# A fused graph network on one core: graph 0 without GpSimd's units, 11 units a graph by VectorE, variance products in groups of four slots

## The reference

```python
hi = x @ W1[:H];  hj = x @ W1[H:]
h = relu(hi[:, :, None, :] + hj[:, None, :, :] + b1)   # every pair (i, j) of nodes
y = h @ W2 + b2
y = layernorm(y, gamma, beta)                          # over the features of each pair
out = einsum('bij,bijh->bih', adj, y)                  # weighted sum over j
x = layernorm(x + out)
```

## Time and profile before

| | |
|---|---|
| median of 3 runs | 2835.23 us (2824.11 to 2839.78) |
| the profiled execution, its own time | 2829.14 us |
| its span, first to last instruction | 2827.5 us |
| mean granted clock of TensorE | 0.990 of full speed |
| GpSimd busy | 2131.9 us, 75% of the span |
| mean rate of the transfers | 202 GB/s |

### The profile page before, as it was taken

One profiled execution on the slowest core, in us unless ns is written; L12 is line 12 of the kernel. 1 busy time (PEld: TensorE's weight loads), 2 busy tenths in 40 slices (PEclk: granted clock), 3 DMA queues, 4 the chain that ended last, 5 costly groups with the idle time before them and its releaser, 6 DMA issues.

```text
span 2827.5 us, 60731 instructions
## 1 busy us (share of the span) xinstructions
PE 2720.4 (96%) x10882; PEld 1133.2 (40%) x10882; DVE 2655.9 (94%) x20561; ACT 2582.0 (91%) x6916; POOL 2131.9 (75%) x3026
## 2 busy tenths in 40 slices
PE   5999999999999999999999999999999999999993
PEld 2343444444444444444434443444444444434442
DVE  1999999999999999999999999999999999999997
ACT  5999999999999999999999999999999999999991
POOL 4777877777877877777777777778777777777772
PEclk9999999999999999999999999999999999999995
DMA  2555455555545545545545554554555554555452
GB/s 81 195 205 233 192 206 232 192 197 233 201 190 233 207 188 234 208 189 224 217 188 209 227 194 191 215 224 191 211 228 191 212 227 191 203 221 206 188 211 104
DMA packets 170235, 571.71 MB, mean 202 GB/s; under 512 B 68608, under 2 KB 104320, under 8 KB 104320
## 3 DMA queue, kind: packets, MB, share of 16 engines
q1 hardware_dynamic: 169856, 567.82, 51.6%
HBM read 555.17 MB, written 8.39 MB: 199 GB/s over the span
## 4 chain that ended last, share of the span: by engine, by line
DVE 61%; DMA 26%; PE 7%; issue 3%; ACT 1%; SPq 1%; POOL 0%; DVEq 0%; POOLq 0%; ACTq 0%
DVE h L653 38%; DMA cb<-c_scratch 19%; DMA c_scratch<-c 6%; DVE h L639 5%; PE y_ps L387 5%; DVE stats L677 3%; DVE gT L653 3%; DVE x L686 3%; DVE mv L680 1%; DVE z_aff L760 1%; PE ss_ps L399 1%; DVE invs L661 1%; DVE z_aff L755 1%; DVE z L747 1%; DVE c L669 1%
## 5 line engine op out<-in xcount | busy, mean ns | idle before, releaser
L387 PE MATMUL y_ps<-h,w2c 128*128 128x512 f32 x4096 | 2041.9, 613 | 55.7 <-DVE h L639 35.5
L653 DVE CUSTOM_DVE_ANT_0 h<-h,cb 128x128 f32<-128x128 f32 x8192 | 1994.0, 288 | 91.8 <-DMA cb<-c_scratch 91.1
L892 POOL TENSOR_SCALAR h<-vT,uT 128x128 f32<-128x128 f32 x2048 | 1698.5, 843 | 174.9 <-ACT vT L516 105.7
L526 ACT ACTIVATE h<-uv_ps,uT 128x128 f32<-128x128 f32 x4800 | 1433.1, 440 | 4.5 <-DVE gT L653 4.4
L536 ACT ACTIVATE sq<-y_ps,b2c_col 128x1024 f32<-128x1024 f32 x1024 | 1191.2, 1163 | 169.1 <-PE y_ps L387 163.3
L387 PEld LDWEIGHTS y_ps<-h,w2c 128*128 128x128 f32 x4096 | 675.4, 190 | 996.1 <-issue 516.2
L653 DVE DVE_READ_ACCUMULATOR2_ANT gT<- 128x1 f32 x8192 | 629.0, 77 | 0.0
L399 PE MATMUL ss_ps<-sq,sel 128*32 128x512 f32 x4096 | 545.5, 605 | 0.0
L880 POOL TENSOR_TENSOR var_eps<-mv,eps_col 128x1 f32<-128x1 f32 x448 | 94.6, 211 | 371.8 <-DVE mv L680 369.8
L639 DVE TENSOR_SCALAR h<-vT,uT 128x128 f32<-128x128 f32 x1216 | 338.6, 292 | 5.5 <-ACT mask_all L581 3.5
L883 POOL TENSOR_TENSOR rs<-var_eps,minus_half 128x1 f32<-128x1 f32 x448 | 301.8, 674 | 35.0
(11 more groups left out here) (100 smaller groups left out, 1485.0 us busy)
## 6 DMA issues: line engine op xcount, KB each, us to landing
cb<-c_scratch SPq DMA_DIRECT2D x512, 1024.0 KB, 8.3
adj_c<-in_adj_dram SPq DMA_DIRECT2D x512, 8.0 KB
devs<-dev_rows SPq DMA_DIRECT2D x512, 8.0 KB
x_in<-in_x_dram SPq DMA_DIRECT2D x64, 64.0 KB, 10.8
c_scratch<-c SPq DMA_DIRECT2D x128, 32.0 KB, 1.5
adj_in<-in_adj_dram SPq DMA_DIRECT2D x64, 64.0 KB, 4.4
x_res<-in_x_dram SPq DMA_DIRECT2D x64, 64.0 KB, 5.2
out_dram<-x SPq DMA_DIRECT2D x64, 64.0 KB, 3.1
```

What stands on the lines that cost most here:

```text
L387: op = pe.matmul(y_ps[:, t % 2, c0:c0 + COLS], w2c[:], h[:, t, c0:c0 + COLS], start=True, stop=True)
L526: op = act.activation(h[:, t, n * P:(n + 1) * P], v, ACT.Relu, bias=uT[:, b, i:i + 1])
L653: op = dve.tensor_tensor_reduce(h[:, t, cols], h[:, t, cols], cb[:, t // 2, c0:c0 + P], 1.0, 0.0, ALU.mult, ALU.add, gT[:, i:i + 1])
L892: op = pool.tensor_scalar(h[:, t, n * P:(n + 1) * P], vT[:, b, :], uT[:, b, i:i + 1], 0.0, ALU.add, ALU.max)
```

## The change

Four things change together.

1. `vector_units(g, t)`: VectorE makes 4 units of each slot in graph 0, and in later graphs one unit in odd slots, none in even ones, and 4 in slot 15 as before: 7 + 4 = 11 a graph where there were 19. ScalarE makes the others of the first six: 6 in even slots, 5 in odd ones, 2 in slot 15, that is 85 a graph where there were 77. GpSimd still makes the last two.
2. `pool_units(g, t)`: in graph 0 GpSimd makes none, and ScalarE makes units 4 to 7.
3. `spread_coefficients`: the first chunk of a half (two slots, 1 MB) goes as two transfers of one slot each, with a semaphore of its own for the first (`cb_first`). `weighted_sum` waits for it at the first slot of a half and for the rest of the chunk at the second.
4. `variances(g, t)`: one visit for four slots (`GROUP` = 4) instead of two, 8 matmuls in a row instead of 4. `sq` becomes a ring of six slots, and its places are counted over graphs.

```diff
@@ -22,7 +22,8 @@
-SQ_RING = 4
+SQ_RING = 6
+GROUP = 4
@@ -37,19 +38,38 @@
-def vector_units(t):
-
-    return BLOCK_UNITS if t == SLOTS - 1 else 1
...
-def act_end(t):
-
-    return DUO_UNITS - (2 if early_unit(t) else 1)
+def vector_units(g, t):
+
+    if g == 0 or t == SLOTS - 1:
+        return BLOCK_UNITS
+    return t % 2
+
+
+def pool_units(g, t):
+
+    if g == 0:
+        return 0
+    return 2
...
+def act_end(g, t):
+
+    return DUO_UNITS - pool_units(g, t)
@@ -319,7 +341,13 @@
-                    sp.dma_start(cb[:, CHUNKS * half + p, :], src.partition_broadcast(P)).then_inc(cb_in[CHUNKS * half + p], 16)
+                    skip = 0
+                    if p == 0:
+                        skip = DUO_UNITS * P
+                        sp.dma_start(cb[:, CHUNKS * half, 0:skip], src[0:skip].partition_broadcast(P)
+                                     ).then_inc(cb_first[half], 16)
+                    sp.dma_start(cb[:, CHUNKS * half + p, skip:], src[skip:].partition_broadcast(P)
+                                 ).then_inc(cb_in[CHUNKS * half + p], 16)
@@ -376,13 +404,14 @@
-                    wait(pe, h_dve, SLOTS * g + t + 1)
-                    if t < SLOTS - 1:
-                        wait(pe, h_act_head, (SLOTS - 1) * g + t + 1)
+                    if vector_units(g, t) > 0:
+                        wait(pe, h_dve, vector_slots(g, t))
+                    if vector_units(g, t) < BLOCK_UNITS:
+                        wait(pe, h_act_head, head_slots(g, t))
                     wait(pe, sq_done, SLOTS * g + t - 1)
                 else:
                     wait(pe, h_act, SLOTS * g + t + 1)
-                    wait(pe, h_pool, SLOTS * g + t + 1)
+                    wait(pe, h_pool, SLOTS * (g - 1) + t + 1)
@@ -390,15 +419,17 @@
-                half, p = t // HALF, (t % HALF) // 2
-                wait(pe, sq_done, SLOTS * g + t + 2)
-                if p == 0:
+                half = t // HALF
+                wait(pe, sq_done, SLOTS * g + t + GROUP)
+                if t % HALF == 0:
                     wait(pe, dev_done, 2 * g + half)
-                for q in range(4):
-                    c0 = (q % 2) * COLS
-                    mm = pe.matmul(ss_ps[32 * q:32 * q + 32, :], sel[:, ROWS - 1 - p:ROWS - 1 - p + 32],
-                                   sq[:, (t + q // 2) % SQ_RING, c0:c0 + COLS],
-                                   start=(p == 0), stop=(p == ROWS - 1))
+                for d in range(GROUP):
+                    p = (t + d) % HALF // 2
+                    for block in range(2):
+                        q = 2 * (d % 2) + block
+                        mm = pe.matmul(ss_ps[32 * q:32 * q + 32, :], sel[:, ROWS - 1 - p:ROWS - 1 - p + 32],
+                                       sq[:, (SLOTS * g + t + d) % SQ_RING, block * COLS:(block + 1) * COLS],
+                                       start=(p == 0), stop=(p == ROWS - 1))
                 mm.then_inc(var_summed, 1)
@@ -493,8 +524,8 @@
-                    sg, t = lagging(graphs, s, START + 3)
-                    if s % 2 == 1 and sg is not None:
+                    sg, t = lagging(graphs, s, START + 1 + GROUP)
+                    if t % GROUP == 0 and sg is not None:
                         variances(sg, t)
@@ -632,18 +663,20 @@
                 if n == 0:
-                    if t % 2 == 0:
+                    if t % HALF == 0:
+                        wait(dve, cb_first[t // HALF], 16 * (g + 1))
+                    elif t % 2 == 0 or t % HALF == 1:
                         wait(dve, cb_in[t // 2], 16 * (g + 1))
```

More of the change, by code:

```diff
@@ L37, with slots_where, vector_slots, head_slots @@
 LATER_SET_UP_SLOT = 2
-def vector_units(t):
-    return BLOCK_UNITS if t == SLOTS - 1 else 1
-def early_unit(t):
-    return True
-def act_end(t):
-    return DUO_UNITS - (2 if early_unit(t) else 1)
+def vector_units(g, t):
[6 more added lines that the diff above has]
+    return 2
+def slots_where(units, g, t):
+    return sum(1 for i in range(SLOTS * g + t + 1) if units(i // SLOTS, i % SLOTS))
+def vector_slots(g, t):
+    return slots_where(lambda g, t: vector_units(g, t) > 0, g, t)
+def head_slots(g, t):
+    return slots_where(lambda g, t: vector_units(g, t) < BLOCK_UNITS, g, t)
+def act_end(g, t):
+    return DUO_UNITS - pool_units(g, t)
 def unit_of(t, n):
@@ L187, in build @@
         cb_in = [sem(f"cb_in{i}") for i in range(2 * CHUNKS)]
+        cb_first = [sem(f"cb_first{i}") for i in range(2)]
         dev_done, inv_done, c_made = sem("dev_done"), sem("inv_done"), sem("c_made")
@@ L311, in store_coefficients @@
                     wait_apart(sp, cb_in[CHUNKS * half + p], 16 * g)
+                wait_apart(sp, cb_first[half], 16 * g)
                 wait_apart(sp, c_stored[half], 16 * g)
@@ L511, in keep_uv @@
                 wait(act, uv_made, g + 1)
-                wait(act, h_dve, SLOTS * (g - 1))
+                wait(act, h_dve, vector_slots(g - 2, SLOTS - 1))
                 wait(act, h_act, SLOTS * (g - 1))
-                wait(act, h_pool, SLOTS * (g - 1))
+                wait(act, h_pool, SLOTS * (g - 2))
                 act.activation(uT[:, b, :], u_ps, ACT.Identity, bias=b1_col[:])
@@ L518, in hidden @@
             def hidden(g, b, t, n):
-                if n == vector_units(t):
+                if n == vector_units(g, t):
                     wait(act, ttr_done, SLOTS * (g - 1) + t + 1)
@@ L528, in hidden @@
                     op.then_inc(h_act_head, 1)
-                if n == act_end(t) - 1:
+                if n == act_end(g, t) - 1:
                     op.then_inc(h_act, 1)
@@ L534, in squares @@
                 wait(act, y_done, SLOTS * g + t + 1)
-                wait(act, var_summed, SLOTS // 2 * g + (t - SQ_RING) // 2 + 1)
-                act.activation(sq[:, t % SQ_RING, :], y_ps[:, t % 2, :], ACT.Square,
+                wait(act, var_summed, (SLOTS * g + t - SQ_RING) // GROUP + 1)
+                act.activation(sq[:, (SLOTS * g + t) % SQ_RING, :], y_ps[:, t % 2, :], ACT.Square,
                                bias=b2c_col[:], scale=float(P) ** -0.5).then_inc(sq_done, 1)
             def deviations(g, half):
-                wait(act, var_summed, SLOTS // 2 * g + HALF // 2 * (half + 1))
+                wait(act, var_summed, SLOTS // GROUP * g + HALF // GROUP * (half + 1))
                 wait(act, devs_in[half], 64 * g)
@@ L606, in iteration @@
                     tail_steps(1, 4)
-                    first = vector_units(ht)
-                    for n in range(first, act_end(ht)):
+                    first = vector_units(hg, ht)
+                    for n in range(first, act_end(hg, ht)):
                         if n == first + 2:
@@ L616, in iteration @@
                             hidden(hg, hb, ht, n)
-                    if act_end(ht) <= first + 2:
+                    if act_end(hg, ht) <= first + 2:
                         tail_steps(4, 6)
@@ L620, in iteration @@
                             keep_uv(new, buf)
-                    if act_end(ht) <= first + 4:
+                    if act_end(hg, ht) <= first + 4:
                         tail_steps(6, 8)
@@ L634, in hidden @@
                     wait(dve, ttr_done, SLOTS * (g - 1) + t + 1)
-                    if t == 0:
+                    if t <= 1:
                         wait(dve, uv_ready, g + 1)
@@ L639, in hidden @@
                 op = dve.tensor_scalar(h[:, t, n * P:(n + 1) * P], vT[:, b, :], uT[:, b, i:i + 1], 0.0, ALU.add, ALU.max)
-                if n == vector_units(t) - 1:
+                if n == vector_units(g, t) - 1:
                     op.then_inc(h_dve, 1)
@@ L825, in iteration @@
                             if hg is not None:
-                                for n in range(vector_units(ht)):
+                                for n in range(vector_units(hg, ht)):
                                     hidden(hg, hb, ht, n)
@@ L904, in iteration @@
                     for k in range(FINE):
-                        if k == 0 and hg is not None:
+                        if k == 0 and hg is not None and pool_units(hg, ht) > 0:
                             hidden(hg, hb, ht, DUO_UNITS - 1)
-                        if k == EARLY_AT and eg is not None and early_unit(et):
+                        if k == EARLY_AT and eg is not None and pool_units(eg, et) > 0:
                             hidden(eg, eb, et, DUO_UNITS - 2)
```

## The result

The changed kernel takes 2875.76 us (median of 4 runs, 2875.19 to 2876.75) against 2834.34 for the kernel before (median of 4, 2824.11 to 2839.78). The ratio is 1.0153, 95% interval 1.0132 to 1.0174: slower by 1.5%. The prediction said 2757 us and a chance of 0.80 for faster. It was wrong, and 2876 is outside its range of 2705 to 2820.

What follows compares the result with a forecast made beforehand. VectorE was taken as full, TensorE and ScalarE as nearly so. From 2829 us, 15 for the start and 0.9 a graph over 63 graphs (57) came off, giving 2757 us, range 2705 to 2820.

Steps and rivals of the forecast that it cites:

- VectorE's lateness: TensorE's waits for VectorE's h in the steady part, 0.6 us a graph, expected back once VectorE makes fewer units.
- What bounds the kernel now: Steady-part reading: VectorE full but for coefficient waits of 1.34 us a graph, TensorE nearly full, a graph 42.84 us.
- the stall of the long visit: TensorE's longer variance visit holds up ScalarE, said to run 1.3 us behind products: charged 0.3 us a graph.
- Part 1, the seams: Entering and leaving TensorE's variance visits: 0.28 us saved a visit, four fewer a graph; 0.6 a graph booked.
- Part 2, ScalarE's units: Eight units a graph move from VectorE to ScalarE: +2.1 us there, ScalarE's need between 40.7 and 42.4 a graph.
- There I expect no gain: Nine slots a graph where ScalarE has almost no gap: added units (1.1 us) use up hidden idle time, gaining nothing.
- Part 3, the split: Half of the first coefficient chunk lands 1.3 us earlier (0 to 2.6), nearly cancelled by later deviations; booked at nothing.
- Part 4, the start: Graph 0 without GpSimd's units: TensorE's stand of 15.23 us goes, gain 15 us, bounds 12 and 17.
- The one given 0.08: Rival, 0.08: ScalarE full at 42.4 a graph plus waits after long visits; 2890 us at 0.4 a visit.
- the packing rival: Rival, 0.15: TensorE and ScalarE, nearly full, work without loss, as read in the start; graph 40.9, time 2694 us.
- The sign of long visits named at the end: Sign of being wrong: squares wait for y over 1.5 us a graph together with TensorE waiting for ScalarE's h.
- the signs of being right: No early TensorE gap, visits 1.85 to 1.95, no h wait, ScalarE 95% or more, VectorE 92% or less, graph 41.5 to 42.2.

Runs made afterwards that it cites:

- e4: Kernel before with only graph 0's units moved from GpSimd to VectorE and ScalarE: 2812.09 us, ratio 0.9932.
- e7: Changed kernel with visits of two slots and 19 VectorE units again, so only the start and the split first chunk are new: 2768.56 us, ratio 0.9793.
- e12: Changed kernel with 19 VectorE units again; start, split and visits of four slots stay: 2808.83 us, ratio 0.9925.
- e1: Changed kernel with visits of two slots and a ring of four again; 11 VectorE units, start and split stay: 2815.05 us, ratio 0.9944.
- e2: Kernel before with only visits of four slots and the ring of six: 2851.38 us, ratio 1.0072.
- e3: Kernel before with only VectorE's units cut to 11 a graph: 2840.53 us, ratio 1.0033.
- e8: e7 with 15 VectorE units a graph, none in every fourth slot: 2770.17 us, ratio 0.9803.
- e9: Changed kernel with ScalarE's deviations behind the first two units of their slot, not ahead of all: 2858.96 us, ratio 1.0101.
- e10: e7 with 15 VectorE units a graph, none in even slots, two or one in odd slots: 2770.82 us, ratio 0.9808.
- e14: e12 with its 19 VectorE units placed so ScalarE makes one less in the slot ahead of a visit, one more in the visit's: 2822.30 us, ratio 0.9979.

## Why the prediction was wrong

In per cent of the kernel before, the path from before to after is: start -0.68 (e4); split -1.39 (e4 to e7); visits of four with 19 units +1.32 (e7 to e12); the eight units +2.28 (e12 to after). That sums to +1.53. The other way round, units first, they are +1.51 (e7 to e1) and +2.09 (e1 to after): each costs more behind the other. On the kernel before, alone, they cost only +0.33 and +0.72. There VectorE's waits for the coefficients stand in some of the same slots (8 and 12 are 0.22 and 0.36 longer than in e7), and the runs bear out that the costs overlap: the split is worth 0.72 a graph with neither part (e4 to e7), 0.35 with the visits (e2 to e12) and 0.12 with the units (e3 to e1).

The same path against the terms of the sum, in us a graph: 0.6 was to come back from VectorE's lateness by the units, and they cost 0.7 to 1.0; the visits were to give 0.6 and take 0.3, and they cost 0.65 to 0.94; the split stood at nothing and gave 0.72. So two steps failed, the stall of the long visit and, by more, the room for ScalarE's units. Under both lies one assumption: that what an engine idles in one slot can be used for work in another.

- **What bounds the kernel now.** The reading of the chain and of VectorE's 16.3 us of idle time was right, but the step "nothing else holds it and it is full" led past its lever: the full engine was held by a transfer 1.34 us a graph, and e7 against e3 shows that this wait, not its units, was what to take away.
- **Part 1, the seams.** Right. A visit of 16 records takes 1.85 against two of 1.00, and entering and leaving cost 0.19 to 0.20: 0.33 saved a visit, at the upper end of 0.19 to 0.33, where 0.28 was taken. TensorE's need did fall to about 40.8 (an estimate: 64 records at 0.43, four visits at 2.05, and 5.1 of other work, which is what e7's full TensorE leaves of 42.12). The saving is real, but no time came of it. The Trainium skill ("TensorEngine Tiling (Array Packing)", Key Properties) has the rule that a change of tiling mode drains the array; the seams of 0.19 to 0.20 agree with it.
- **Part 1, the stall.** This step failed: "it runs some 1.3 us behind a finished product", hence a charge of 0.3 a graph. In the trace of after the squares of the visit slots start 0.51, 0.62, 0.84 and 0.63 behind the end of their products (medians, ends as modelled), not 1.3. The longer visit is paid at 0.52 to 0.72 a time (e7 to e12), four times a graph, not 0.3 once. And the slots freed of a visit can't use all that they gain (1.8 of 4.8 us), since ScalarE's 2.25 stands under them.
- **Part 2, ScalarE's units.** The price of a unit was right, 0.25 start to start. The step that failed is the next one: ScalarE's idle 2.4 us a graph was taken for room. It isn't: it lies in the slots where TensorE is the longer, and the added units fall as well on slots where ScalarE is. "There I expect no gain" for nine slots should have read a loss of up to 0.25 a slot. In after both engines idle, ScalarE 19.6 of 500 us and TensorE 20.3. VectorE's lateness did go (78.9 to 11.4 of weight load waits), but the 0.6 did not come back: TensorE's wait for ScalarE took its place, 1.57 a graph. The Trainium skill ("ScalarE: Activation LUTs", Rules for kernel authors), which puts relu on VectorE, was weighed at 8 x 0.045 us. The eight units cost 9 us alone (e3), 43 behind e7 and 65 behind e12, and four of them nothing (e8), so the runs bear its advice out where ScalarE shares the pace, though for another reason than the price of the instruction.
- **Part 3, the split.** Booked at nothing, worth 39 us. The half did not land 1.3 earlier but 0.6 (4.1 against 4.7, medians), yet the loop was what ended last, so each tenth counted, twice a graph. After hides this gain: with the eight units the split is worth only 0.12 a graph. The delay of the deviations behind the long visit is real, 15 us (e9).
- **Part 4, the start.** Right in kind, 19 instead of 15. TensorE's 12th record of products ends at 36.93 before (29.54 and 7.39) and near 20.0 after (23.42 less eight records at 0.43), 16.9 earlier: the stand of 15.2 and part of the slow records behind it, 7.39 for ten. Behind the stand the records start 0.85 apart, later 0.43. The profile prints a granted clock of 1.00, full speed, for both, so why they are slow stays open.
- **The rivals.** The one given 0.08, ScalarE the bound with waits for y after each long visit, is what happened: its stall per visit was to decide at 0.25 and it gave 2890 for 0.4. Its picture of a ScalarE full at 42.4 was too simple, since ScalarE is 96% busy. "Two nearly full engines ran without loss", said for the packing rival, was read in graph 0, where no later layers make slots uneven and TensorE alone set the pace. The sign of long visits named at the end, squares waiting for y over 1.5 us a graph together with TensorE waiting for h, came out by half: TensorE waits 1.57 for h, but the squares wait only 1.25, less than the 2.4 before. Of the signs of being right, all that tell of work came true (the start, visits of 1.85, VectorE's lateness gone, ScalarE at 95% or more of the stretch, VectorE at 91%) and only the one that tells of time, the graph, did not.

Why slots 2 to 14 differ among themselves (slot 10 keeps 2.85, slot 14 falls to 2.51) probably follows the later layers' work on each engine; I did not test it slot by slot.

## What to carry to other kernels

When two nearly full engines hand work back and forth over two buffers, take the time over as many slots as the buffer spans, here two neighbours, as the longer of the two engines in each such stretch, and not the sums of their busy time over a whole round. An uneven cut with a smaller sum was slower here (e12 against e7), and idle time where the other engine is longer is no room. Single slots are too short for this: moving units between neighbours gave nothing (e10, e14). That the number of buffers sets the length of the stretch is inferred from these two; no run has another number. Work on one engine that saves its own set-up by coming in larger lumps must be held against what the buffer covers (here 0.5 to 0.8 us for a lump 0.85 longer). And where the chain ends in an engine with a transfer before it, look first at the latency of that transfer: here half a megabyte taken out of the first chunk was worth 39 us, the start 19.

## What the hardware showed that I had not expected

Halving the first transfer from 1 MB to 512 KB took its landing only from 4.7 to 4.1 us, though whole chunks in the queue do land 2.6 to 2.8 us apart (4.7, 7.3, 10.0 and 12.8 us behind the first issue in e4). Whether most of the 4.1 is a fixed time, or the second half, issued 0.4 us behind, takes bandwidth from the first, no run shows, since none sends the half alone. The one transfer more isn't free: the second to fourth chunks of e7 are there after 8.1, 10.8 and 13.5 us, 0.8 later each, but VectorE hardly waits for them (2.6 us in the whole span).

A wait can sit inside what the trace counts as busy. After's TensorE shows 20.3 us of idle time in 500, 1.8 a graph, but by the estimate of its need it stands 3.0 a graph (43.77 less 40.8). The rest must be in what is printed as busy, if the estimate holds. Against e7 the records in the stretch (1945 and 2024) and the busy time (479.7 and 499.0) both fall by 3.9%, as the graph grows, and neither shows that a graph needs 1.3 us less of TensorE.
